# Dummy transposes at two places of an eight-stage graph and expert network on one core

## The chip, the cores and the metric

The kernel runs on one core of a Trainium2 chip, in one launch. The metric is the device time of one execution in microseconds, lower is better. It is given as the median of several executions.

## The reference, cut to what matters

The input is a matrix `x` of 128 rows (nodes, or tokens) by 512 columns in float32, and 2048 edges (`src`, `dst`, `edge_weight`). Eight layers follow each other, each on the normalised rows, each added to `x`:

```python
x = x + _L0_gnn_ref(_layernorm(x), ...)   # similarity-weighted graph sweeps
x = x + _L0_ffn_ref(_layernorm(x), ...)   # 8 experts, top 2, gelu
x = x + _L1_gnn_ref(_layernorm(x), ...)   # relu(((1+eps) x + agg) W1' + b1) W2' + b2, layer norm
x = x + _L1_ffn_ref(_layernorm(x), ...)   # 8 experts of width 32, top 1
x = x + _L2_gnn_ref(_layernorm(x), ...)   # 4 experts of two graph convolutions, top 2
x = x + _L2_ffn_ref(_layernorm(x), ...)   # 8 leaves of a soft tree, gelu
x = x + _L3_gnn_ref(_layernorm(x), ...)   # edge attention, then a small dense block, two layer norms
x = x + _L3_ffn_ref(_layernorm(x), ...)   # 8 experts, top 2, silu, and a shared expert
```

So each layer begins with the mean and variance of the rows that the layer before has just finished, and nothing of its dense work can start before them.

## The kernel before, in words

**Products.** All large weights lie in DRAM as 156 chunks of 512 by 512 float32 (1 MB each), in the order of use. SyncE loads them into eight slots `raw`; a slot is loaded again when VectorE has read it. ScalarE rounds a chunk to `w_hi` (`round_chunk`, L359, in halves L367) and VectorE takes the rest `w_lo` (`split_chunk`, L973, in parts L980). Both have four slots, which come free when TensorE has used the chunk. The rows that are multiplied are split in the same way, into `x_hi` (ScalarE, L373) and `x_lo` (VectorE, L955), or `hT_hi` and `hT_lo`. `product` (L612) is twelve matmuls of 512 columns on TensorE: four of high by high, four of high rows by low weights, four of low rows by high weights.

**Turning.** The matmul wants the rows' features on the partitions, so `turn` (L624) transposes a 128x512 tile in four pieces of 128x128, and ScalarE copies the result out of the bank `tp`.

**The order of the work.** Each engine's instructions stand in the program in the order in which it runs them; semaphores hold the engines together. Nothing is planned at run time.

**Between two layers** there is a chain of small steps. VectorE adds the last expert to `X`, takes the statistics (`statistics`, L932 and L933, which raises the semaphore `var`), GpSimd makes the reciprocal root (L316, L317, semaphore `rstd`), VectorE writes the normalised rows `XN` (`normalise_x`, L951, semaphore `xn`). TensorE waits for `xn`, turns `XN` (`turn_x`), ScalarE rounds to `x_hi`, and the first product starts. `keep_clock(n)` (L631) issues `n` transposes of the identity into a bank that nobody reads, ahead of the wait for `xn`. The table `BRIDGE` says how many stand ahead of which layer.

**The second graph layer (`l1g`)** does not use `turn_x`. After the last product of the layer before (`L0F`) TensorE puts two bias rows into the banks `pre[0]` and `pre[1]` (L772, L773), passes a wait for `c_ds` (the edge counts, made long before), waits for `xn`, and multiplies `XN` by the matrix `agg1`: eight matmuls of 128 columns (L777), whose result is the aggregated and turned tile in one. Then come `x_hi`, a product, a ReLU (L495), a `turn`, `hT_hi` (L381), and the second product, whose statistics VectorE takes straight from the bank (L932).

**Ahead of the last dense layer (`l3f`)** TensorE's last act in the layer before is a small product for `y[0]` (L912). VectorE adds it (L1324), takes the statistics `l3g_out`, centres and scales (L938), waits for the reciprocal root, adds into `X` (L942), takes the statistics `l3f` of that, and after a second reciprocal root writes `XN` (L951). So two statistics stand between L912 and the turning. During this TensorE runs 44 of the dummy transposes and then waits for `xn`. In the last dense layer a product (`pre[0]`), the router's small matmuls (`logits`, L642) and the other products follow.

Of the kernel before, what the change touches and what calls it, by code (L numbers as in the profile page):

```python
# [26 lines left out]
RAW_SLOTS = 8  # L27
SPLIT_SLOTS = 4

BRIDGE = {"l0g": 0, "l0f": 4, "l1f": 37, "l2g": 23, "l2f": 30, "l3g": 28, "l3f": 44}  # L30
SIM_AT = 12
FIRST_HOTS = 2
EARLY_COUNTS = 4
# [75 lines left out]
def nth(stage, tag):  # L109

    return STAGES[stage].index(tag) + 1
# [12 lines left out]
def gnn_ffn_kernel(nc, A, out):  # L124
    with ExitStack() as ctx:
# [8 lines left out]
        def sm(name):  # L134

            if name not in named:
                named[name] = ctx.enter_context(nc.semaphore("s_" + name))
            return named[name]
# [458 lines left out]
        def _(pe):  # L597
# [24 lines left out]
            def turn(dst, src, done, n=KC):  # L622
                for c in range(n):
                    last = pe.transpose(dst[:, c * P:(c + 1) * P], src[:, c * P:(c + 1) * P], ident[:])  # L624
                last.then_inc(done, 1)

            def keep_clock(n):


                for _ in range(n):  # L630
                    pe.transpose(wt[1][:, 0:P], ident[:], ident[:])  # L631

            def turn_x(tag):
                keep_clock(BRIDGE[tag])
                pe.wait_ge(sm("xn"), nth("xn", tag))
                turn(tp, XN, sm("xt"))

            def logits(tag, w, E):

                pe.wait_ge(sm("xt32"), nth("xt32", tag))  # L640
                for c in range(KC):
                    last = pe.matmul(ms[:, 0:E], XT[:, c], w[:, c, 0:E], start=c == 0, stop=c == KC - 1)  # L642
                last.then_inc(sm("logits"), 1)
# [128 lines left out]
            pe.matmul(pre[0][:], ones[0:1, :], brow[0:1, :], start=True, stop=False)  # L772
            pe.matmul(pre[1][:], ones[32:33, :], brow[32:33, :], start=True, stop=False)  # L773
            pe.wait_ge(sm("c_ds"), 1)
            pe.wait_ge(sm("xn"), nth("xn", "l1g"))
            for c in range(KC):
                last = pe.matmul(tp[:, c * P:(c + 1) * P], XN[:, c * P:(c + 1) * P], agg1[:], start=True, stop=True)  # L777
# [133 lines left out]
            pe.wait_ge(sm("l3g_f1s"), 1)  # L911
            pe.matmul(y[0][:], fT[:], b2[:], start=True, stop=True).then_inc(sm("l3g_f2"), 1)  # L912

            turn_x("l3f")
            pipeline(L3F, lambda: logits("l3f", rwT[:, 1], E8), False)

# [504 lines left out]
```

## Time and profile before

| | |
|---|---|
| median of three executions | 591.35 us |
| lowest and highest | 589.77 and 594.08 us |
| span of the profiled execution, first to last instruction | 590.4 us |
| TensorE busy | 557.9 us, 94% |
| VectorE busy | 490.8 us, 83% |
| ScalarE busy | 412.2 us, 70% |
| GpSimd busy | 15.7 us, 3% |
| mean granted TensorE clock | 0.988 |
| moved by DMA | 168.06 MB, 285 GB/s |

The profiled execution is a fourth one; for it the page gives the span alone. Its span lies 0.95 us below the median of the three timed ones. The row PEclk of the page gives TensorE's granted clock in forty slices: 1.00 is 2.4 GHz, 0.50 is 1.2 GHz, and a slice in between holds some of each.

### The profile page before, as it was taken

The numbers are of one execution on the slowest core, as the hardware profiler recorded it, in microseconds if no ns is written. First come the engines' busy times: TensorE is split into PE (matmuls) and PEld (weight loads), VectorE is DVE, ScalarE is ACT, GpSimd is POOL, SyncE is SP. The second block draws the span as 40 slices with busy tenths as digits, with TensorE's granted clock in tenths as the row PEclk, the third lists the DMA queues.
The fourth block names the chain that finished last, engine by engine and source line by source line (L and its number), as shares of the span: only waits on it lengthen the run. The fifth ranks groups of instructions, "written<-read, shape, count | busy, mean of one in ns | idle before, by whom it ended". The sixth has DMA issues, their size and how long they took to land.

```text
span 590.4 us, 8259 instructions
## 1 busy us (share of the span) xinstructions
PE 557.9 (94%) x2747; PEld 455.5 (77%) x2747; DVE 490.8 (83%) x475; ACT 412.2 (70%) x411; POOL 15.7 (3%) x40
## 2 busy tenths in 40 slices
PE   5898999997899998999999999999998799999997
PEld 4676888884678887688888888888877588888886
DVE  7799898994659986888988989889987759998996
ACT  4787878772159876878778787787842447878783
POOL 3100000000100000000000000000000100000000
PEclk9999999998899999999999999999999989999999
DMA  8689989995257985689989989998971248999830
GB/s 286 233 313 422 380 328 347 344 329 197 73 172 291 378 304 197 260 325 347 352 330 345 334 345 352 325 354 327 356 284 74 76 163 316 354 353 340 341 121 19
DMA packets 26861, 168.06 MB, mean 285 GB/s; under 512 B 5228, under 2 KB 5357, under 8 KB 6856
## 3 DMA queue, kind: packets, MB, share of 16 engines
q1 hardware_dynamic: 25430, 165.72, 74.5%
q10 hardware_dynamic: 1410, 2.07, 1.1%
q8 instruction: 13, 0.21, 0.1%
q14 instruction: 8, 0.07, 0.0%
HBM read 167.51 MB, written 0.26 MB: 284 GB/s over the span
## 4 chain that ended last, share of the span: by engine, by line
PE 79%; DVE 10%; ACT 5%; issue 3%; POOL 2%; DMA 1%; SPq 0%; POOLq 0%; DVEq 0%; ACTq 0%
PE pre L612 33%; PE y L612 33%; PE tp L624 6%; DVE w_lo L973 3%; ACT w_hi L359 2%; PE pre L619 2%; DVE st L932 1%; POOL rstd L317 1%; PE y L711 1%; DMA ends<-in_edge_weight 1%; ACT L417 1%; DVE XN L951 1%; PE wt L831 1%; PE pre L727 1%; POOL rstd L316 1%
## 5 line engine op out<-in xcount | busy, mean ns | idle before, releaser
L973 DVE TENSOR_TENSOR w_lo<-raw,w_hi 128x2048 fp32r<-128x2048 f32 x151 | 340.0, 2287 | 48.4 <-ACT w_hi L359 48.0
L359 ACT ACTIVATE w_hi<-raw 128x2048 fp32r<-128x2048 f32 x152 | 285.4, 1915 | 0.0
L422 ACT ACTIVATE hT_hi<-tp 128x512 fp32r<-128x512 f32 x66 | 39.5, 599 | 82.0 <-PE tp L624 82.0
L612 PE MATMUL pre<-w_hi,x_hi 128*128 128x512 f32 x292 | 81.4, 401 | 3.7 <-ACT x_hi L373 2.9
L612 PE MATMUL y<-w_hi,hT_hi 128*128 128x512 f32 x280 | 81.7, 413 | 0.0
L612 PE MATMUL pre<-w_lo,x_hi 128*128 128x512 f32 x292 | 80.2, 397 | 1.4 <-DVE w_lo L973 0.9
L612 PE MATMUL pre<-w_hi,x_lo 128*128 128x512 f32 x292 | 78.9, 392 | 0.0
L612 PE MATMUL y<-w_lo,hT_hi 128*128 128x512 f32 x280 | 75.7, 392 | 0.5 <-DVE w_lo L973 0.4
L612 PE MATMUL y<-w_hi,hT_lo 128*128 128x512 f32 x280 | 75.2, 390 | 0.0
L612 PEld LDWEIGHTS pre<-w_hi,x_hi 128*128 128x128 f32 x292 | 54.9, 192 | 17.1 <-issue 3.6
L612 PEld LDWEIGHTS pre<-w_lo,x_hi 128*128 128x128 f32 x292 | 55.6, 192 | 14.8 <-DVE w_lo L973 2.3
L612 PEld LDWEIGHTS pre<-w_hi,x_lo 128*128 128x128 f32 x292 | 55.4, 190 | 11.9
L612 PEld LDWEIGHTS y<-w_lo,hT_hi 128*128 128x128 f32 x280 | 52.4, 188 | 13.4 <-DVE w_lo L973 1.3
L612 PEld LDWEIGHTS y<-w_hi,hT_lo 128*128 128x128 f32 x280 | 52.6, 188 | 11.6
L612 PEld LDWEIGHTS y<-w_hi,hT_hi 128*128 128x128 f32 x280 | 47.9, 189 | 6.6
L624 PE MATMUL tp<-ident,h 128*128 128x128 f32 x298 | 44.8, 272 | 2.7 <-ACT h L495 0.7
L1031 DVE TENSOR_TENSOR hT_lo<-tp,hT_hi 128x512 fp32r<-128x512 f32 x66 | 45.0, 682 | 2.2 <-ACT hT_hi L422 2.2
L624 PEld LDWEIGHTS tp<-ident,h 128*128 128x128 f32 x298 | 36.5, 139 | 13.4 <-issue 1.8
L417 ACT ACTIVATE h<-pre 128x512 f32<-128x512 f32 x66 | 39.2, 594 | 0.1
L631 PE MATMUL wt<-ident 128*128 128x128 f32 x223 | 26.4, 273 | 0.0
L631 PEld LDWEIGHTS wt<-ident 128*128 128x128 f32 x223 | 24.7, 141 | 2.0 <-issue 1.6
L1058 DVE SCALAR_TENSOR_TENSOR X<-y,gates,X 128x512 f32<-128x512 f32 x33 | 24.5, 741 | 2.1 <-PE y L612 2.1
(252 smaller groups left out, 385.8 us busy)
## 6 DMA issues: line engine op xcount, KB each, us to landing
raw<-in_chunks SPq DMA_DIRECT2D x156, 1024.0 KB, 5.5
side<-in_L_gnn_emb ACTq DMA_DIRECT2D x1, 512.0 KB, 3.9
affine<-in_L_ffn_W SPq DMA_DIRECT2D x1, 512.0 KB, 7.3
side<-in_L_ffn_W SPq DMA_DIRECT2D x1, 512.0 KB, 10.1
affine<-in_L_gnn_ln_g ACTq DMA_DIRECT2D x2, 256.0 KB, 4.4
affine<-in_L_gnn_ln_b ACTq DMA_DIRECT2D x2, 256.0 KB, 4.9
X<-in_x ACTq DMA_DIRECT2D x1, 256.0 KB, 2.8
affine<-in_L_gnn_gamma SPq DMA_DIRECT2D x1, 256.0 KB, 5.5
```

What stands on the lines that cost most here:

```text
L316: link(pool.tensor_scalar(rstd[:, 0:1], mv[:, 1:2], LN_EPS, None, ALU.add))
L317: pool.tensor_tensor(rstd[:, 1:2], rstd[:, 0:1], mhalf[:], ALU.pow).then_inc(sm("rstd"), 1)
L359: act.activation(w_hi[:, g % SPLIT_SLOTS], raw[:, g % RAW_SLOTS], ACT.Copy).then_inc(w_hi_ready, 4)
L417: act.activation(h[:, s % 2], pre[s % 2][:], pipe.act).then_inc(sm("gate_ready") if s < pipe.lead else h_ready, 1)
L422: act.activation(hT_hi[:, (s - 1) % 2], tp[:].rearrange("p (c n) -> p c n", n=P), ACT.Copy).then_inc(hT_hi_ready, 1)
L612: last = pe.matmul(dst, xs[:, k], ws[:, k], start=start and i == 0, stop=stop and i == len(passes) - 1 and bias is None)
L619: last = pe.matmul(dst, rows, halves, start=False, stop=True)
L624: last = pe.transpose(dst[:, c * P:(c + 1) * P], src[:, c * P:(c + 1) * P], ident[:])
L631: pe.transpose(wt[1][:, 0:P], ident[:], ident[:])
L973: dve.tensor_tensor(w_lo[:, i], raw[:, g % RAW_SLOTS], w_hi[:, i].bitcast(F32), ALU.subtract).then_inc(w_lo_ready, 4)
L1031: dve.tensor_tensor(hT_lo[:, (s - 1) % 2], chunks4(tp), hT_hi[:, (s - 1) % 2].bitcast(F32), ALU.subtract).then_inc(hT_lo_ready, 1)
L1058: dve.scalar_tensor_tensor(out=X[:], in0=y[q % 2][:], scalar=gate, in1=X[:], op0=ALU.mult, op1=ALU.add).then_inc(y_summed, 1)
```

## The change

The table gets an entry `l1g` of 30, and these transposes are issued between the wait for `c_ds` and the wait for `xn`. Ahead of the last dense layer the 44 transposes become 15, a wait for the statistics `l3g_out`, 33, a wait for the statistics `l3f`, and 14. In all 48 transposes (30 and 18) and two waits are added on TensorE. No other engine's program changes.

```diff
-BRIDGE = {"l0g": 0, "l0f": 4, "l1f": 37, "l2g": 23, "l2f": 30, "l3g": 28, "l3f": 44}
+BRIDGE = {"l0g": 0, "l0f": 4, "l1g": 30, "l1f": 37, "l2g": 23, "l2f": 30, "l3g": 28, "l3f": 14}
+BRIDGE_L3G_OUT = (15, 33)
...
             pe.wait_ge(sm("c_ds"), 1)
+            keep_clock(BRIDGE["l1g"])
             pe.wait_ge(sm("xn"), nth("xn", "l1g"))
...
             pe.matmul(y[0][:], fT[:], b2[:], start=True, stop=True).then_inc(sm("l3g_f2"), 1)
 
+            keep_clock(BRIDGE_L3G_OUT[0])
+            pe.wait_ge(sm("var"), nth("var", "l3g_out"))
+            keep_clock(BRIDGE_L3G_OUT[1])
+            pe.wait_ge(sm("var"), nth("var", "l3f"))
             turn_x("l3f")
             pipeline(L3F, lambda: logits("l3f", rwT[:, 1], E8), False)
```

## Rows read from the trace of the kernel before

**Rows 1.** The page: busy times, the chain by engine, the group of dummy transposes.

```profile
PE 557.9 (94%) x2747; PEld 455.5 (77%) x2747; DVE 490.8 (83%) x475; ACT 412.2 (70%) x411; POOL 15.7 (3%) x40
...
PE 79%; DVE 10%; ACT 5%; issue 3%; POOL 2%; DMA 1%; SPq 0%; POOLq 0%; DVEq 0%; ACTq 0%
...
L631 PE MATMUL wt<-ident 128*128 128x128 f32 x223 | 26.4, 273 | 0.0
```

**Rows 2.** The page: the granted TensorE clock in forty slices of the span.

```profile
PEclk9999999998899999999999999999999989999999
```

**Rows 3.** Windows around l1g: length, busy of five engines, PEclk, DMA share, GB/s.

```profile
134.00:136.00 2.00, 0.45 (x4) 0.00 (x0) 1.06 (x3) 0.00 (x0) 0.70 (x2) 1.00 0.96 332
...
138.00:140.00 2.00, 1.37 (x3) 1.16 (x4) 1.47 (x2) 0.58 (x1) 0.00 (x0) 0.62 0.00 0
140.00:142.00 2.00, 2.00 (x6) 1.53 (x5) 0.00 (x0) 0.00 (x0) 0.00 (x0) 0.53 0.88 270
...
144.00:146.00 2.00, 1.31 (x8) 0.93 (x8) 0.85 (x2) 1.48 (x2) 0.00 (x0) 1.00 0.00 0
```

**Rows 4.** Timeline of PE ahead of l1g: start, us, line, tiles, count, idle before.

```profile
133.86 0.59 PE L773 MATMUL pre<-brow,ones 1*128 1x512 f32 x1
136.81 1.13 PE L777 MATMUL tp<-agg,XN 128*128 128x128 f32 x8 [2.37 <-DVE XN L951]
```

**Rows 5.** The chain that ended last, in l1g: start, us, what.

```profile
136.12 0.56 DVE XN L951
...
138.63 4.52 PE pre L612 x12
...
143.82 0.67 PE tp L624 x4
...
145.17 3.07 PE pre L612 x12
```

**Rows 6.** Windows around the start of l3f.

```profile
464.00:466.00 2.00, 2.00 (x20) 2.00 (x19) 1.50 (x3) 0.70 (x1) 1.68 (x2) 1.00 0.94 397
...
472.00:474.00 2.00, 2.00 (x6) 1.52 (x6) 2.00 (x1) 0.49 (x1) 0.00 (x0) 0.50 0.77 311
...
478.00:480.00 2.00, 2.00 (x10) 1.66 (x9) 1.35 (x7) 1.95 (x4) 0.00 (x0) 1.00 0.22 86
```

**Rows 7.** Timeline of PE ahead of l3f.

```profile
461.50 0.59 PE L912 MATMUL y<-b,fT 33*128 33x512 f32 x1
462.02 5.02 PE L631 MATMUL wt<-ident 128*128 128x128 f32 x44
```

**Rows 8.** The chain that ended last, at the start of l3f.

```profile
463.65 0.19 DVE mv L933
...
467.32 0.19 DVE mv L933
...
468.84 0.56 DVE XN L951
...
469.44 1.07 PE tp L624 x4
...
471.19 5.41 PE pre L612 x12
```

**Rows 9.** Timeline of PE at two other bridges, ahead of l1f and of l3g.

```profile
148.78 4.26 PE L631 MATMUL wt<-ident 128*128 128x128 f32 x37
...
427.13 3.22 PE L631 MATMUL wt<-ident 128*128 128x128 f32 x28
430.62 0.66 PE L624 MATMUL tp<-ident,XN 128*128 128x128 f32 x4 [0.27 <-DVE XN L951]
```

**Rows 10.** Windows of l1f, of the start of l3g, and of the last dense layer.

```profile
156.00:158.00 2.00, 2.00 (x6) 1.66 (x7) 1.07 (x5) 0.00 (x0) 0.00 (x0) 0.50 0.45 86
...
432.00:434.00 2.00, 2.00 (x9) 1.63 (x10) 2.00 (x3) 0.00 (x0) 0.00 (x0) 1.00 0.19 37
...
477.00:589.00 112.00, 110.10 (x520) 90.47 (x519) 96.90 (x76) 82.70 (x73) 0.00 (x0) 1.00 0.67 250
```

## The prediction

> **What bounds the kernel now.** I read the page's busy times and its chain first. TensorE works 94% of the span and holds 79% of the chain that ended last [rows 1], so time is won where TensorE idles or runs slow. The page's clock row shows where it runs slow: slices 10, 11 and 33 (counted from one) are below full speed [rows 2]. Windows over these slices and the PE timeline give three places.
>
> First, l1g. After the bias rows TensorE idles 2.37 us until XN is there [rows 4]; the clock is still 1.00 then, but falls to 0.50 within 138 to 140 us and is back before 144 [rows 3]. The first product of l1g takes 4.52 us in the chain, the second, at full clock, 3.07 us for the same twelve matmuls [rows 5]. Second, l1f, after a bridge of 37 transposes: 0.50 in 156 to 158 us [rows 9, 10]. The change does not touch it. Third, l3f. The 44 transposes end at 462.02 + 5.02 = 467.04 [rows 7], the turning starts at 469.44 [rows 8], so TensorE idles 2.40 us; the clock is at 0.50 in 472 to 474 and at 1.00 again in 478 to 480 [rows 6]. The chain shows turning at 1.07 us and the first product at 5.41 us [rows 8].
>
> **What the change does in l1g.** It adds 30 transposes between the bias rows and the wait for XN. Their pace: 44 took 5.02 us [rows 7], and one record lasts 0.27 us [rows 1], so (5.02 - 0.27) / 43 = 0.110 us each, and by the bridge of 28, (3.22 - 0.27) / 27 = 0.109 [rows 9]. Their start: the last float32 matmul of 512 columns ahead of the l3f bridge starts at 461.50, the first transpose at 462.02, 0.52 later [rows 7]. Here the last such matmul starts at 133.86 [rows 4], so they begin at 134.38 and need 30 x 0.110 = 3.3 us, until about 137.7. The matmuls on XN could start at 136.81 [rows 4]. **So this bridge is too long by 0.85 us, and that stands on the chain**: the 30 block TensorE's own queue, nothing else waits for it meanwhile, and everything of l1g moves by it. Bounds: 0.7 us (28 steps at the pace of the 28, with overlap at the end) to 1.0 us.
>
> What it gives back is the slow clock. If the clock stays at 1.00, the first product takes 3.07 instead of 4.52 us: 1.45 us. The low part of the rows is wanted only at the ninth matmul, 8 x 3.07 / 12 = 2.0 us after the start, so VectorE should have it ready and no new wait arises. Net for l1g: 1.45 - 0.85 = 0.6 us won. Bounds: from 0.85 us lost (clock falls all the same) to 1.2 us won.
>
> **What it does ahead of l3f.** 15 transposes from 462.02 last until about 463.7; the statistics l3g_out are done at 463.65 + 0.19 = 463.84 [rows 8]. The 33 then run from about 463.9 for 3.65 us to 467.6; the statistics l3f are there at 467.51 [rows 8]. The 14 take 1.55 us, until 469.15; XN ends at 469.40 and the turning starts at 469.44 [rows 8]. The three groups fit into waits that are there anyway, with 0.25 us to spare, so I cost the 18 added transposes and the two waits at nothing. The cover is the VectorE and GpSimd chain of two statistics and two roots; were it 0.3 us shorter, the rest would go onto the path. Behind each new wait on TensorE stand only dummies, and XN is written after both statistics, so no useful work is held back.
>
> The idle of 2.40 us shrinks to 0.3 us at most in one piece. If the clock then holds: turning takes 0.66 us, as at l3g [rows 9], instead of 1.07, a gain of 0.41; the first product 3.07 [rows 5] instead of 5.41 [rows 8], a gain of 2.34. Sum 2.75 us. Is it given back behind? The next products need chunks that are already split, the router's steps on VectorE and ScalarE hang on the product itself and move with it, and from 477 to 589 us TensorE is busy 110.10 of 112 us while VectorE has 96.90 and ScalarE 82.70 [rows 10]: TensorE bounds the rest, and the DMA share is 0.67. So it reaches the end. Bounds: nothing, if the clock falls anyway, to 3.2 us, if the late part of the router's matmuls gains too.
>
> **Does the bridge hold the clock?** The nearest rows are those of l3g: 28 transposes, 0.27 us idle, turning, then the product in 432 to 434 us at 1.00 [rows 9, 10]. That is just the form that l3f gets. From 464 to 466 us TensorE did nothing but transposes and kept 1.00 [rows 6]. Against it speaks l1f: 37 transposes, and yet 0.50 three microseconds after they end [rows 9, 10]; but there only four transposes and matmuls of 8 columns follow, with pauses, before the fall. In l1g eight matmuls of 128 columns follow, then a product; l3f has four transposes, then a product.
>
> The Trainium skill, page TensorE: Matmul & The Clock Gate, section Part 4: PE-mode transpose, says the opposite of what the change lives on: a transpose is not counted as TensorE activity as a matmul is, and full clock does not engage for it. By that rule both bridges would do nothing for the clock. The windows of 464 to 466 and 432 to 434 us disagree with it, so its case gets a small chance.
>
> **The sum.** 0.6 + 2.75 = 3.35 us off the profiled span of 590.4, giving 587.05. The median lies 0.95 us above that span, so 588.0. The three timed runs spread over 4.3 us, and the place at which the clock falls after an idle need not be the same in each: in l1g it fell about 1.7 us after work had resumed (0.62 over 138 to 140 is 0.5 us at full and the rest at half [rows 3], work resumed at 136.81 [rows 4]), in l3f already in the turning, which took 1.07 us [rows 8]. A run whose slow stretch at l3f is as short as that of l1g has about 1.45 us to win there instead of 2.75. I take 0.2 off for such runs: **588.2 us**.
>
> **The rivals.**
> (a) *The fall moves on instead of going away.* l1g has two more short pauses around the turning at 143.82 [rows 5], and there is at l1f a phase of short work with pauses that did drop the clock. If the second product of l1g then takes 4.52 instead of 3.07, l1g loses 0.85 and l3f wins 2.75: 1.9 us won, 589.4 us. Against: these pauses lie in 144 to 146 us at 1.00 [rows 3]. Chance 0.12.
> (b) *Slower: the dummies do not hold the clock.* Then l1g pays the overrun of 0.85 us and wins nothing, l3f wins nothing, and the three groups may add 0.1: 592.3 us. It sits in the product at the start of l3f, and decides if that product is at 0.50 again; slower than before from the point at which both bridges return less than the 0.85 us overrun. This is where the skill's rule leads. Chance 0.06.
> (c) *The slow stretch at l3f is mostly short in the timed runs.* Then l3f gives 1.45 us, l1g 0.6: 2.05 us won, 589.3 us. Chance 0.15.
> (d) *The change does less than it says*: the semaphore of the statistics is already past its count, or the groups run together, so that a gap stays before XN as now. 44 became 62 transposes, so the gap would be 2.40 - 18 x 0.110 = 0.4 us even then; the clock holds, the result is that of the forecast. No price of its own.
> (e) *More than forecast*: timed runs paid more for the slow clock than the profiled one, as their highest, 594.08, hints. Then 4.5 us or more are won: 586.5 us. Chance 0.12.
> The forecast has 0.55.
>
> **The numbers.** Most likely 588.2 us. The range takes in (a), (c), (e), the bounds of the overrun and a median that may stand 0.5 us off in so few runs: 586.1 to 590.5 us. A measurement of this kernel cannot tell less than about 1% (5.9 us) from no change. Faster than 585.4 us would need all slow stretches gone at more than their price here: 0.05. Slower than 597.3 us has no row behind it, only chance: 0.02. Within: 0.93.
>
> **What the profile after would show.** Right: the matmuls on XN in l1g start about 0.85 us after the record of XN allows, with no idle before them; the first product of l1g takes 3.1 us; the turning ahead of l3f 0.66 us and the first product 3.1 us; the clock row has one dip, at l1f. Wrong: 0.50 in a window of l1g or l3f; a PE wait for w_lo in the first products of l3f, which would mean VectorE gives the gain back; l1g's transposes ending before XN, which would mean that the overrun is not there.

## The result and the profile after

| | before | after |
|---|---|---|
| median | 592.61 us (20 runs) | 588.92 us (20 runs) |
| lowest, highest | 589.77, 594.76 | 586.30, 591.24 |
| span of the profiled execution | 590.4 us | 588.4 us |
| time of the profiled execution | not given | 590.08 us |
| mean granted clock in it | 0.988 | 0.996 |

The ratio after to before is 0.9941, 95% interval 0.9925 to 0.9958: the change wins 3.5 us, between 2.5 and 4.4. Forecast were 3.15 to 3.35 us, and 588.2 us. With seventeen more runs the median of the kernel before is 1.26 us higher than that of the first three.

In the code after, line numbers are one more than before up to the bias rows, two more behind them, and six more in VectorE's part: L613 is `product`, L625 `turn`, L632 `keep_clock`, L774 the bias row, L779 the matmuls on XN, L938 the statistics.

The page of the kernel after (busy times, granted clock in forty slices):

```profile
PE 559.5 (95%) x2795; PEld 457.7 (78%) x2795; DVE 491.0 (83%) x475; ACT 412.2 (70%) x411; POOL 15.7 (3%) x40
...
PEclk9899999999999999999999999999999999999999
```

Slices 10, 11 and 33, which were low [rows 2], are at 9; slice 2 is now low. TensorE has 48 matmul records more, the dummies.

**l1g.** The timeline of PE (answers to [rows 4]):

```profile
136.68 0.59 PE L774 MATMUL pre<-brow,ones 1*128 1x512 f32 x1
137.20 3.49 PE L632 MATMUL wt<-ident 128*128 128x128 f32 x30
140.53 1.06 PE L779 MATMUL tp<-agg,XN 128*128 128x128 f32 x8
```

The chain of the kernel after in l1g (answers to [rows 5]), the dummies now on it:

```profile
137.27 3.42 PE wt L632 x30
...
142.27 3.04 PE pre L613 x12
...
147.33 3.04 PE pre L613 x12
```

Windows of the kernel after over l1g (answers to [rows 3]):

```profile
140.00:142.00 2.00, 1.59 (x15) 1.40 (x13) 1.69 (x1) 0.38 (x1) 0.00 (x0) 1.00 0.45 184
142.00:144.00 2.00, 1.73 (x8) 1.42 (x8) 0.69 (x1) 0.22 (x1) 0.00 (x0) 1.00 0.50 131
```

From the last bias matmul to the matmuls on XN there were 2.95 us [rows 4], there are now 140.53 - 136.68 = 3.85: 0.90 us of overrun, with no idle ahead of L779. The first product went from 4.52 us [rows 5] to 3.04.

**Ahead of l3f.** The timeline of PE (answers to [rows 7]) and then the chain (answers to [rows 8]), both of the kernel after:

```profile
462.63 7.29 PE L632 MATMUL wt<-ident 128*128 128x128 f32 x62
470.06 0.66 PE L625 MATMUL tp<-ident,XN 128*128 128x128 f32 x4
...
475.08 1.19 PE L613 MATMUL y<-w_hi,x_hi 128*128 128x512 f32 x4
```

```profile
464.26 0.19 DVE mv L939
...
467.93 0.19 DVE mv L939
...
469.46 0.56 DVE XN L957
...
471.40 3.03 PE pre L613 x12
```

The 62 end at 469.92, 0.14 us before the turning starts, and XN is there at 470.02. The product takes 3.03 us instead of 5.41. Windows of the kernel after, over the product and over the rest of the last layer (answers to [rows 6, 10]):

```profile
472.00:474.00 2.00, 2.00 (x10) 1.65 (x9) 2.00 (x2) 0.60 (x1) 0.00 (x0) 1.00 0.75 217
...
475.00:587.00 112.00, 110.05 (x518) 90.30 (x518) 96.90 (x76) 82.65 (x73) 0.00 (x0) 1.00 0.70 256
```

**Where the two spans differ.** To cut the span I need some more marks. Of the kernel before, VectorE's statistics of l1g's second product and its addition at the end of l1f, then PE's second product of l3f:

```profile
148.33 0.70 DVE L932 BATCH_NORM_STATS2 st<-pre 128x6 f32<-128x512 f32 x1 [1.89 <-PE pre L612]
...
163.60 0.69 DVE L1207 TENSOR_TENSOR X<-X,y 128x512 f32<-128x512 f32 x1 [1.18 <-PE y L802]
```

```profile
477.25 1.16 PE L612 MATMUL y<-w_hi,x_hi 128*128 128x512 f32 x4
```

The same two VectorE rows of the kernel after:

```profile
150.47 0.70 DVE L938 BATCH_NORM_STATS2 st<-pre 128x6 f32<-128x512 f32 x1 [1.87 <-PE pre L613]
...
164.28 0.69 DVE L1213 TENSOR_TENSOR X<-X,y 128x512 f32<-128x512 f32 x1 [1.17 <-PE y L804]
```

| stretch | before, us | after, us | difference |
|---|---|---|---|
| start to the last bias matmul | 133.86 | 136.68 | +2.82 |
| to the statistics of l1g's second product | 14.47 | 13.79 | -0.68 |
| to the addition at the end of l1f | 15.27 | 13.81 | -1.46 |
| to the first dummy ahead of l3f | 298.42 | 298.35 | -0.07 |
| to the second product of l3f | 15.23 | 12.45 | -2.78 |
| to the end of the span | 113.2 | 113.3 | +0.1 |

The change touches the second and the fifth line: 3.46 us. The first and third are not its work. (Of the 0.68 us in the second line, 1.48 - 0.90 = 0.58 are the product and the overrun; the rest is spread over the matmuls on XN and the second product, which are each a little shorter.) In the first layer, where nothing was changed, the profiled execution of the kernel after had a slow stretch that the other had not. PE in the first layer, before, and then after:

```profile
19.75 1.03 PE L744 MATMUL pre<-XN,mat_b 128*128 128x256 f32 x4
20.62 1.02 PE L747 MATMUL wt<-h,mat_b 128*128 128x512 f32 x2
```

```profile
21.05 1.92 PE L745 MATMUL pre<-XN,mat_b 128*128 128x256 f32 x4
22.75 1.70 PE L748 MATMUL wt<-h,mat_b 128*128 128x512 f32 x2
```

The window of the kernel after over it:

```profile
22.00:24.00 2.00, 2.00 (x5) 1.25 (x4) 0.85 (x2) 2.00 (x2) 0.00 (x0) 0.50 0.27 111
```

That stretch accounts for about 1.7 us. The rest of the 2.82 us lies in the load of the edge weights, which took 4.16 us in one chain and 5.01 in the other, and in the first matmuls (0.3 us). At l1f it was the other way round: before it was at 0.50 [rows 10], after it was not. So the span of one execution, 2.0 us shorter, would have told too little; the stretches tell 3.46 us, and the medians of twenty 3.69.

### The profile page after: what moved, and what is told of

Same layout as the page of the kernel before. It is cut to its first block, busy times and chain, and to the rows that moved or that the text cites. A ratio compares the mean times of both kernels' runs of the same rounds, so it can differ in the third digit from the quotient of the medians.

```text
span 588.4 us, 8354 instructions
## 1 busy us (share of the span) xinstructions
PE 559.5 (95%) x2795; PEld 457.7 (78%) x2795; DVE 491.0 (83%) x475; ACT 412.2 (70%) x411; POOL 15.7 (3%) x40
## 4 chain that ended last, share of the span: by engine, by line
PE 80%; DVE 10%; ACT 4%; issue 3%; POOL 1%; DMA 1%; SPq 0%; POOLq 0%; DVEq 0%; ACTq 0%
PE y L613 33%; PE pre L613 33%; PE tp L625 6%; DVE w_lo L979 3%; ACT w_hi L360 2%; PE pre L620 2%; DVE st L938 1%; POOL rstd L318 1%; DMA ends<-in_edge_weight 1%; PE y L712 1%; ACT L418 1%; PE pre L728 1%; PE wt L833 1%; PE wt L632 1%; DVE XN L957 1%
## 5 line engine op out<-in xcount | busy, mean ns | idle before, releaser
L613 PE MATMUL pre<-w_hi,x_hi 128*128 128x512 f32 x292 | 79.6, 394 | 3.7 <-ACT x_hi L374 2.9
L613 PE MATMUL y<-w_hi,hT_hi 128*128 128x512 f32 x280 | 81.7, 413 | 0.0
L613 PE MATMUL pre<-w_lo,x_hi 128*128 128x512 f32 x292 | 78.7, 391 | 1.4 <-DVE w_lo L979 0.9
L613 PE MATMUL pre<-w_hi,x_lo 128*128 128x512 f32 x292 | 78.2, 390 | 0.0
L613 PE MATMUL y<-w_lo,hT_hi 128*128 128x512 f32 x280 | 75.8, 392 | 0.4 <-DVE w_lo L979 0.4
L613 PE MATMUL y<-w_hi,hT_lo 128*128 128x512 f32 x280 | 75.2, 390 | 0.0
L613 PEld LDWEIGHTS pre<-w_hi,x_hi 128*128 128x128 f32 x292 | 53.9, 188 | 16.8 <-issue 3.6
L613 PEld LDWEIGHTS pre<-w_lo,x_hi 128*128 128x128 f32 x292 | 54.5, 188 | 14.3 <-DVE w_lo L979 2.3
L613 PEld LDWEIGHTS pre<-w_hi,x_lo 128*128 128x128 f32 x292 | 54.8, 188 | 11.6
L613 PEld LDWEIGHTS y<-w_lo,hT_hi 128*128 128x128 f32 x280 | 52.4, 188 | 13.3 <-DVE w_lo L979 1.3
L613 PEld LDWEIGHTS y<-w_hi,hT_lo 128*128 128x128 f32 x280 | 52.6, 188 | 11.6
L613 PEld LDWEIGHTS y<-w_hi,hT_hi 128*128 128x128 f32 x280 | 47.9, 189 | 6.6
L625 PE MATMUL tp<-ident,h 128*128 128x128 f32 x298 | 44.9, 272 | 2.4 <-ACT h L496 0.7
L625 PEld LDWEIGHTS tp<-ident,h 128*128 128x128 f32 x298 | 36.5, 139 | 12.9 <-issue 1.3
L632 PEld LDWEIGHTS wt<-ident 128*128 128x128 f32 x271 | 29.9, 141 | 3.1 <-issue 2.4
L632 PE MATMUL wt<-ident 128*128 128x128 f32 x271 | 32.2, 274 | 0.0
```

What stands on the lines that cost most here:

```text
L613: last = pe.matmul(dst, xs[:, k], ws[:, k], start=start and i == 0, stop=stop and i == len(passes) - 1 and bias is None)
```

## The experiments

All ratios are to the kernel before, run beside it on the same chip; not all experiments ran on one chip, but the four medians of the kernel before lie within 592.4 and 592.7 us. The column of the clock is the mean granted clock of the profiled execution; `l1g`, `l1f` and `l3f` are the lengths of the second, third and fifth stretch of the table above in the profiled execution, worked out in the same way (for e5 and e7, where no dummy stands there, the fifth begins 0.52 us after the small product's second record, as in the others).

| kernel | median, us (runs) | ratio, 95% | l1g | l1f | l3f | clock |
|---|---|---|---|---|---|---|
| before, first profile | 592.61 (20) | 1 | 14.47 | 15.27 | 15.23 | 0.988 |
| after | 588.92 (20) | 0.9941 (0.9925 to 0.9958) | 13.79 | 13.81 | 12.45 | 0.996 |
| e1 l1g alone | 591.46 (12) | 0.9977 (0.9957 to 0.9997) | 13.79 | 15.36 | 14.01 | 0.994 |
| e2 l3f alone | 590.82 (12) | 0.9967 (0.9939 to 0.9995) | 14.36 | 13.82 | 12.48 | 0.996 |
| e3 22 at l1g | 587.53 (6) | 0.9918 (0.9892 to 0.9944) | 12.91 | 14.88 | 12.45 | 0.997 |
| e4 62 in one | 588.30 (6) | 0.9932 (0.9907 to 0.9958) | 13.79 | 13.82 | 12.44 | 0.999 |
| e5 none at l3f | 592.12 (12) | 0.9988 (0.9969 to 1.0007) | 13.79 | 15.12 | 15.65 | 0.985 |
| e6 matmul dummies | 610.91 (4) | 1.0315 (1.0285 to 1.0346) | 17.28 | 17.30 | 18.91 | 1.000 |
| e7 44, late | 588.96 (10) | 0.9939 (0.9917 to 0.9962) | 13.79 | 13.81 | 13.27 | 0.994 |
| e8 all filled | 587.26 (6) | 0.9918 (0.989 to 0.9947) | 12.92 | 13.82 | 12.46 | 1.000 |
| e9 l1f filled | 587.42 (6) | 0.992 (0.9889 to 0.9951) | 12.92 | 13.82 | 12.48 | 1.000 |
| e10 early too | 585.85 (6) | 0.9896 (0.9869 to 0.9922) | 12.91 | 14.73 | 12.45 | 0.997 |
| e11 11 at l1g | 589.33 (10) | 0.994 (0.9917 to 0.9963) | 12.92 | 15.39 | 12.45 | 0.996 |

### Each bridge by itself

e1 is the change without its second half; e2 is the change without its first.

```diff
# e1, against the kernel after
-"l3f": 14}
+"l3f": 44}
-            keep_clock(BRIDGE_L3G_OUT[0])
-            pe.wait_ge(sm("var"), nth("var", "l3g_out"))
-            keep_clock(BRIDGE_L3G_OUT[1])
-            pe.wait_ge(sm("var"), nth("var", "l3f"))
# e2, against the kernel after
-            keep_clock(BRIDGE["l1g"])
```

> Only the 30 transposes ahead of l1g; 44 in one group ahead of l3f, as before. Theory (two bridges that work each for itself; 0.85 us of overrun against 1.45 us of slow clock in l1g, 2.75 us in l3f): 0.6 us under the kernel before, ratio 0.999; in its trace the first product of l1g takes 3.05 us, the first product of l3f over 4 us, with 0.50 in the windows there. Rival (the fall only moves on within l1g): 0.85 us over before, with 0.50 in the second product of l1g. Rival (the l1g bridge carries the whole gain, the l3f groups nothing): 3.4 us under before.

> Only the three groups ahead of l3f; no transposes ahead of l1g, as before. Theory: 2.75 us under before, ratio 0.995; first product of l3f 3.05 us, first product of l1g some 4.5 us at 0.50. Rival (the dummies do not hold the clock and the measured gain is that of l1g or of chance at the start): no difference from before, and 0.50 at the start of l3f.

PE of e1 at l3f, and its window over the product:

```profile
461.67 5.02 PE L632 MATMUL wt<-ident 128*128 128x128 f32 x44
469.09 0.66 PE L625 MATMUL tp<-ident,XN 128*128 128x128 f32 x4 [2.40 <-DVE XN L953]
470.44 1.89 PE L613 MATMUL pre<-w_hi,x_hi 128*128 128x512 f32 x4 [0.69 <-ACT x_hi L374]
```

```profile
472.00:474.00 2.00, 2.00 (x6) 1.52 (x6) 1.30 (x1) 0.00 (x0) 0.00 (x0) 0.50 0.92 389
```

PE of e2 at l1g, its window there, and PE at l3f:

```profile
137.20 1.13 PE L778 MATMUL tp<-agg,XN 128*128 128x128 f32 x8 [2.37 <-DVE XN L956]
139.02 2.08 PE L613 MATMUL pre<-w_hi,x_hi 128*128 128x512 f32 x4 [0.69 <-ACT x_hi L374]
```

```profile
140.00:142.00 2.00, 2.00 (x6) 1.57 (x5) 0.00 (x0) 0.00 (x0) 0.00 (x0) 0.50 0.69 197
```

```profile
469.58 1.21 PE L613 MATMUL pre<-w_hi,x_hi 128*128 128x512 f32 x4 [0.69 <-ACT x_hi L374]
```

Both profiled executions show what was expected, and neither bridge needs the other. Where a place is left as it was, TensorE idles 2.37 or 2.40 us and the product after it meets 0.50; where the change is made, it does not. The gains by ratio are 1.4 us (0.2 to 2.5) for l1g and 2.0 us (0.3 to 3.6) for l3f, together about what the whole change wins. The stretches give the split more sharply, but of one execution each, and that of e2 (588.35 us) is the third fastest of its twelve: four others have a mean clock of 0.986 to 0.988, as low as the kernel before, with l3f bridged. Some executions without the bridge at l1g so lose more to slow clock than this trace shows; none of them has a trace, so where they lose it stays open. The traces show something else: at l3f the clock fell later in e1, after the turning, and the stretch is 1.56 us longer than after the change, not 2.78. Cut into short windows, the trace of the kernel before is at 0.50 from about 469.6 to 476.4 us, 6.8 us in all, that of e1 from about 470.7 to 474.1, half as long. So the price of one idle is not one number; 1.56 and 2.78 were both seen.

### How many ahead of l1g

```diff
# e3, against the kernel after          # e11
-"l1g": 30                              -"l1g": 30
+"l1g": 22                              +"l1g": 11
```

> The changed kernel with 22 instead of 30 transposes ahead of l1g. Theory (the eight last ones stand in the way of XN): eight fewer are 0.88 us less, the matmuls on XN start 3.0 us after the last bias matmul instead of 3.85, the clock stays at 1.00 through both products: 0.85 us under the changed kernel, about 4.3 under before, ratio 0.993. Rival (XN comes later on other runs and the 30 are no overrun, or 22 are too few to hold the clock): no gain over the changed kernel, or a first product of 4.5 us.

> The changed kernel with 11 instead of 30 transposes ahead of l1g, so that they end about 1.2 us before XN. Theory (a shorter bridge holds too, as long as the rest of the idle is near the 1 us that stands elsewhere at full clock): matmuls on XN 2.95 us after the last bias matmul, no 0.50 in l1g, the time of the kernel with 22. Rival (22 are needed): first or second product of l1g over 4 us in this look, 1.5 us over the kernel with 22.

PE of e3, then of e11, in l1g:

```profile
135.16 2.62 PE L632 MATMUL wt<-ident 128*128 128x128 f32 x22
137.62 1.06 PE L779 MATMUL tp<-agg,XN 128*128 128x128 f32 x8
```

```profile
135.22 1.42 PE L632 MATMUL wt<-ident 128*128 128x128 f32 x11
137.56 1.16 PE L779 MATMUL tp<-agg,XN 128*128 128x128 f32 x8 [0.92 <-DVE XN L957]
```

In e3 the matmuls on XN come 0.88 us sooner after the bias matmul (2.97 instead of 3.85) and the stretch is 0.88 us shorter, at full clock: the last eight transposes were pure overrun. It is the trace that shows this; the medians lie 1.4 us apart, but the intervals of the two ratios overlap. In e11 the profiled execution had full clock in l1g too, with 0.92 us idle. But its ten runs have a median of 589.33, 1.8 us over e3 as its rival had it, and five of them a mean clock of 0.994 or less, where none of e3's six is below 0.996. Eleven seem to hold in some executions and not in others; that is read from means, no trace shows the fall, and the intervals of e3 and e11 overlap.

### What the three groups and the waits are for

```diff
# e4                      # e5                     # e7
-"l3f": 14}               -"l3f": 14}              -BRIDGE_L3G_OUT = (15, 33)
+"l3f": 62}               +"l3f": 0}               +BRIDGE_L3G_OUT = (0, 30)
# e4 and e5 also:
-            keep_clock(BRIDGE_L3G_OUT[0])
-            pe.wait_ge(sm("var"), nth("var", "l3g_out"))
-            keep_clock(BRIDGE_L3G_OUT[1])
-            pe.wait_ge(sm("var"), nth("var", "l3f"))
```

> The changed kernel with all 62 transposes ahead of l3f in one group and without the two waits for statistics. Theory (what counts is that TensorE does not idle for long before XN, not the waits): they end about 62 x 0.110 = 6.8 us after they start, some 0.6 us before XN; clock 1.00, first product 3.05 us; same time as the changed kernel within 0.3 us. Rival (the waits are what does it, since a gap of 0.6 us right before XN still lets the clock fall): first product over 4 us and 2 to 3 us over the changed kernel.

> The changed kernel (30 ahead of l1g) with no dummy transposes at all ahead of l3f; TensorE idles from the small product to XN, some 7.4 us. Theory (the clock falls after a long idle, and the 44 of the kernel before, which left 2.4 us idle, bought little or nothing): 0.50 from before the turning on; turning 1.07 us, first product of l3f between 4.4 and 5.4 us, over the changed kernel by 2 to 3 us, as if the 44 stood there. Rival (an idle of 7.4 us costs much more than one of 2.4, so that the 44 held part of it): over the changed kernel by more than 3.5 us.

> The changed kernel without the first 15 transposes ahead of l3f and with 30 instead of 33 behind the first wait: 44 in all, as many as in the kernel before, but they run until just before XN, and the idle of 1.9 us lies ahead of them. Theory (what counts is what TensorE did just before and in the first work, not the number of dummies): 1.00 throughout, turning 0.66 us, first product of l3f 3.05 us, the time of the changed kernel. Rival (an idle of about 2 us drops the clock wherever it lies): 0.50 within the dummies or in the product, 1 to 3 us over the changed kernel.

PE of e4, then of e5, then of e7, ahead of l3f:

```profile
459.57 6.99 PE L632 MATMUL wt<-ident 128*128 128x128 f32 x62
466.99 0.66 PE L625 MATMUL tp<-ident,XN 128*128 128x128 f32 x4 [0.44 <-DVE XN L953]
```

```profile
468.26 1.11 PE L625 MATMUL tp<-ident,XN 128*128 128x128 f32 x4 [7.35 <-DVE XN L953]
470.06 2.07 PE L613 MATMUL pre<-w_hi,x_hi 128*128 128x512 f32 x4 [0.69 <-ACT x_hi L374]
```

```profile
463.91 6.58 PE L632 MATMUL wt<-ident 128*128 128x128 f32 x44 [1.79 <-DVE mv L939]
470.33 0.60 PE L625 MATMUL tp<-ident,XN 128*128 128x128 f32 x4
```

Windows of e7 over its dummies:

```profile
464.00:466.00 2.00, 2.00 (x10) 2.00 (x11) 1.50 (x3) 0.73 (x1) 1.71 (x2) 0.50 1.01 426
466.00:468.00 2.00, 2.00 (x15) 2.00 (x14) 1.93 (x4) 0.00 (x0) 0.39 (x1) 0.71 0.01 4
468.00:470.00 2.00, 2.00 (x20) 2.00 (x19) 1.23 (x3) 0.00 (x0) 0.75 (x2) 1.00 0.00 0
```

**e4**: one group of 62 gives the same stretch, 12.44 us, with 0.44 us idle. The waits and the grouping bring nothing by themselves; it is the number that fills the wait. **e5**: without any dummy the stretch is 15.65 us (3.2 over the change, where 2 to 3 were expected), 0.4 more than with 44 in the profiled execution of the kernel before, but 1.6 more than with the same 44 in e1. So the old 44, which stopped 2.40 us short, bought nearly nothing in one execution and half of the price in another; the medians of e5 and e1, 592.12 and 591.46, don't tell how much on the whole. **e7**: my theory fell. In the 1.79 us of idle ahead of the dummies, just before they began, the clock fell (0.85 in 463.6 to 463.8 us, 0.50 behind it); they took 6.58 instead of 5.02 us, ran past XN, and the stretch is 0.82 us longer. The slow stretch was spent on dummies and the product ran at full clock. The clock rose again while TensorE ran nothing but transposes: 0.50 in 464 to 466 us, 1.00 in 468 to 470, and the dummies last until 470.49. That costs 0.82 us where in the product it cost 1.56 or 2.78. The medians of e7 and of the change are alike, 588.96 and 588.92, so such a loss in each execution is not shown.

### Do transposes count as activity

```diff
# e6
-                    pe.transpose(wt[1][:, 0:P], ident[:], ident[:])
+                    pe.matmul(wt[1][:, 0:P], ident[:], ident[:], start=True, stop=True)
```

> The changed kernel in which every dummy is a plain matmul of the identity by the identity instead of a transpose, in the same numbers and places. Theory (the dummies hold the clock because TensorE streams, and a float32 transpose streams as a matmul does): same times per dummy if a float32 matmul of 128 columns takes as long (0.11 us each), same products, the time of the changed kernel within 0.5 us. If the matmul takes twice as long, 0.22 us each, the dummies overrun XN everywhere and it is 5 us or more slower, at full clock. Rival (the Trainium skill, TensorE: Matmul & The Clock Gate, Part 4: a transpose does not count as activity): the matmul dummies hold the clock where the transposes did not, above all at l1f.

PE of e6 in l1g:

```profile
135.41 6.96 PE L632 MATMUL wt<-ident 128*128 128x128 f32 x60
```

The thirty matmuls stand as sixty records: a float32 matmul has two, a transpose one, and they take 0.23 us against 0.11. Every bridge overran and the kernel took 610.91 us at full clock throughout. That says nothing for the rival, since with no idle left behind the bridges dummies of either kind may have kept the clock, and the transposes had held it in l1g and l3f in every trace of a kernel that has them to the end. Whether matmuls of the same length would hold it better at l1f was not tested.

### The places that the change leaves

```diff
# e9, against the kernel after
-"l1g": 30, "l1f": 37
+"l1g": 22, "l1f": 42
             turn_x("l1f")
+            keep_clock(6)
...
# e8: e9, and in the first layer
+            keep_clock(5)
             counted_edges(range(EARLY_COUNTS))
+            keep_clock(3)
             pe.wait_ge(sm("l0g_a"), 1)
             pe.transpose(ms[:, 0:P], mat_a[:], ident[:]).then_inc(sm("l0g_aT"), 1)
+            keep_clock(4)
# e10: e8, and
-"l0g": 0
+"l0g": 24
             for i in range(2):
+                if i:
+                    keep_clock(5)
```

> The changed kernel with 22 ahead of l1g, 42 instead of 37 ahead of l1f, 6 between the turning and the router of l1f, and 5, 3 and 4 in the pauses of the first layer (ahead of the counted edges, behind the first four of them, behind the transpose of the weight matrix). Theory (the clock also falls at l1f and in the first layer in a part of the executions, 1.5 and 1.7 us each where it does): no window at 0.50 before the end; 0.88 us less than the changed kernel for l1g and 1 to 1.5 us less in the median for the rest, so 2 us under the changed kernel, 5.7 under before, ratio 0.990, and a narrower spread of runs. Rival (the added dummies stand in the way of what they wait for, or the clock falls there all the same): no less than the kernel with 22 alone, 0.992.

> The kernel with 22 ahead of l1g, and besides 42 instead of 37 ahead of l1f and 6 between the turning and the router of l1f; nothing added in the first layer. Theory (the pauses of l1f are what lets the clock fall there in about half of the executions, for 1.1 to 1.5 us): from the first statistics of l1g to the end of l1f as long as where the clock did not fall, no 0.50 in l1f; about 0.7 us in the median under the kernel with 22 alone. Rival (the 11 added stand in the way of XN or XT): l1f 0.3 to 1 us longer at full clock.

> The kernel with all pauses filled (22, 42 and 6, and 5, 3 and 4 in the first layer) with two groups more: 24 ahead of the very first turning, while TensorE idles for 7 us, and 5 between the sweeps of the first layer. Theory (the first matmuls run at half clock, 0.22 us per float32 matmul of 128 columns instead of 0.11, because TensorE had been idle, and the remaining slow stretch lies there): the sixteen matmuls of the first layer's similarity take 2.0 us instead of 2.8 to 3.8, 1 to 2 us less than the kernel with all pauses filled, some 585.5 us in the median, ratio 0.988. Rival (the start waits for the edges' DMAs and XN in any case, and the early dummies come too soon or run at half clock themselves and end after XN): no gain or up to 1 us more.

PE of e10 in the first layer, then its window at l1f:

```profile
2.06 4.60 PE L632 MATMUL wt<-ident 128*128 128x128 f32 x24 [2.06 <-POOL iota_t L311]
8.11 0.66 PE L625 MATMUL tp<-ident,XN 128*128 128x128 f32 x4 [1.44 <-DVE XN L963]
...
9.45 2.05 PE L728 MATMUL pre<-XT,side 128*128 128x128 f32 x16 [0.24 <-ACT XT L460]
...
15.02 1.39 PE L712 MATMUL y<-affine,raw 128*128 128x128 f32 x6 [0.70 <-DVE affine L1094]
```

```profile
160.00:162.00 2.00, 2.00 (x7) 1.17 (x6) 0.69 (x1) 0.00 (x0) 0.00 (x0) 0.50 0.74 213
```

e8 and e9 show a profile at 1.000 throughout, but half of the six runs of each have 0.996 or 0.997 and are 2 to 3 us longer. Neither median is clear of e3's, so the gains expected of the filled pauses did not show. e10 is the fastest, 585.85 us: the 24 early dummies are slow themselves (4.60 us, where the 22 of e3 took 2.62), the turning then takes 0.66 us, and L728 takes 2.05 us. Without them the same group took 3.78 us in the profile of the change, where PE's record begins:

```profile
8.11 1.09 PE L625 MATMUL tp<-ident,XN 128*128 128x128 f32 x4 [8.11 <-DVE XN L957]
...
9.88 3.78 PE L728 MATMUL pre<-XT,side 128*128 128x128 f32 x16
```

The microsecond so won is not on the path in this execution: TensorE then waits 0.70 us for VectorE's one-hot matrices (`affine`), and the last bias matmul stands at 133.66 us, where e4 has 133.63 and e8 133.72 without the early dummies. So my reason for e10 is not borne out by its trace, though its six runs, 585.65 to 587.08 us, lie closest together of all kernels but e6; why its median is 1.4 us under e8's stays open, and six runs of each hardly tell the two apart (the intervals of the ratios overlap). In this execution the clock also fell at l1f, late in the layer, in spite of its filled pauses, and cost 0.9 us. The rival of e9 is out, since l1f is no longer than at full clock (13.82), but that those pauses decide it is not shown either: in e2, e4 and e7 the clock held at l1f with the pauses as they were.

## Why the prediction was right

**The bound.** TensorE's chain carried both places to the end: what was won at l1g and l3f stayed won, and the 298 and 113 us of dense work behind them are the same within 0.2 us. That the gain is one of the clock shows beyond the single traces: the twenty runs of the change have mean clocks of 0.994 to 1.000, the 63 runs of the kernel before beside the experiments 0.977 to 0.994, and the twelve of e5, without a bridge at l3f, 0.984 to 0.991.

**l1g.** Overrun forecast 0.85 us, measured 0.90; slow clock forecast 1.45, measured 4.52 - 3.04 = 1.48; net forecast 0.6, measured 0.58 from these two and 0.68 over the stretch. e3 shows the overrun by taking it away.

**l3f.** Forecast 2.75 us, measured 2.78: the turning 1.07 to 0.66, the product 5.41 to 3.03. The 18 more transposes cost nothing, as said; the margin before XN was 0.1 us and not 0.25.

**The sum.** 3.35 forecast, 3.46 in the stretches, 3.69 between the medians. The correction of 0.2 us for executions with a shorter slow stretch went the wrong way or was too fine to see, though e1 shows that such executions exist. The time itself, 588.92, is 0.7 us above the 588.2 forecast, and that lies in the step from span to median: I took 0.95 us from a median of three runs that was 1.26 us low. In every run on record the time is 1.7 to 1.9 us more than the span, so the profiled execution of the kernel before took about 592.1 us, and 592.1 - 3.35 = 588.75. That 588.2 came so near all the same is in part luck. The prediction also put at 1% what a measurement can tell; twenty runs on each side told 0.6%, give or take 0.17.

**Rivals.** (a), the fall moves on, is out: both products of l1g take 3.04 us in the change, in e1 and in e3. (b), the dummies don't hold the clock, is out by e2 and e4, and with it, in this case, what the Trainium skill says in TensorE: Matmul & The Clock Gate, Part 4: PE-mode transpose, that a transpose is not counted as activity; in e7 the clock even rose from 0.50 to 1.00 while nothing but transposes ran. (c) was half right: e1 has the short slow stretch, 1.56 us, but the 2.05 us that it gave for the median lie below the interval. (d) is settled by e4, where the grouping makes no difference. (e), 4.5 us or more, lies just above the interval, which ends at 4.4.

**What was missed.** I said that the clock row after would have one dip, at l1f, and the first layer would stay as it was. The profile has its dip in the first layer and none at l1f. I took the three slow places of one execution for the slow places of the kernel. The profiled executions show l1f slow in before, e1, e3, e5, e10 and e11, and not in after, e2, e4, e7, e8 and e9. And I did not look at the first layer at all, where the sixteen records of L728 (L727 before) take 3.53 us before, 3.78 after, 2.82 in e8 and 2.92 in e9, but 2.05 in e10.

## What to carry to other kernels

A bridge of dummy work pays if it ends as the awaited tile arrives: here one that stopped 2.4 us short bought 0.4 us in one execution and 1.6 in another, of 3.2, and one that ran 0.9 us over gave most of its gain back, so cut its number by the pace in the trace (0.11 us per float32 transpose here). Where some idle must remain, ahead of the dummies it cost less (0.82 us in e7's trace) than ahead of the product (1.56 and 2.78), though no median shows that difference. Judge such a change by the stretches that it touches and by many runs, since the untouched stretches moved by 2.8 and 1.5 us between two profiles.

## What the runs showed of the hardware

- The clock does not fall in the same places in each execution of one kernel. Twenty runs of the change spread over 4.9 us, with mean clocks from 0.994 to 1.000; of e8's six runs, the three at 1.000 took 585.4 to 586.3 us, the three at 0.996 or 0.997 took 588.2 to 588.6. Those 2 to 3 us are more than one slow stretch like that of the first layer costs (1.7 us); what the rest is stays open.
- At l3f the clock fell in the turning in one execution and in the product behind it in another (before and e1), for the same idle of 2.40 us ahead of it. Prices of 2.78 and 1.56 us.
- The clock rose from 0.50 to 1.00 while TensorE ran only float32 transposes (e7, between 466 and 468 us).
- A float32 transpose of 128x128 took 0.11 us and one record, a float32 matmul of that size 0.23 us and two. The eight records of L777, which I took for eight matmuls, are four.
- The granted clock in the page's first slice is doubtful: it says full, while L728's sixteen records took 3.78 us in the kernel after and 2.05 in e10, where TensorE had worked before them. That those matmuls ran at half clock is inferred from the pace alone.
